# Sixteen-head attention on one core: the next head's incidence products are issued ahead of this head's scores below the diagonal

## The reference

```python
std_logits = jnp.einsum('bhqd,bhkd->bhqk', q, k) * scale
...
incidence = jnp.einsum('bqhp,bkhp->bhqk', read_lines, J_write)
decays = jax.nn.sigmoid(decay_logits)
...
weights = decays[:, None, None] ** diffs_pos[None] * past[None].astype(x.dtype)
bias = incidence * weights[None] * bias_scale[None, :, None, None]
logits = std_logits + bias
...
logits = jnp.where(causal_mask[None, None], -jnp.inf, logits)
attn = jax.nn.softmax(logits, axis=-1)
out = jnp.einsum('bhqk,bhkd->bqhd', attn, v).reshape(B, T, D)
```

## Time and profile before

| | |
|---|---|
| median of three runs | 1004.08 us (1004.01 to 1008.88) |
| the profiled execution | 1001.47 us, span 1000.2 us |
| mean granted TensorE clock | 0.949 |
| busy share of the span | PE 86%, PEld 53%, DVE 73%, ACT 66%, POOL 41% |
| chain of waits that ended last | PE 53%, DVE 8%, issue 3%, ACT 3% |
| first and last reduction of the maxima (L1821) | starts at 325.85 and 771.62 us |

### The profile page before, as it was taken

How to read it: one execution, slowest core, us unless ns; L and a number is a source line. 1 busy time by engine, 2 the same in 40 slices (tenths; PEclk the granted TensorE clock), 3 DMA queues, 4 the chain that set the end, 5 groups by cost and what they waited for, 6 DMA issues and landing times.

```text
span 1000.2 us, 25506 instructions
## 1 busy us (share of the span) xinstructions
PE 857.0 (86%) x9999; PEld 527.1 (53%) x9999; DVE 732.9 (73%) x1794; ACT 656.5 (66%) x1154; POOL 407.3 (41%) x667
## 2 busy tenths in 40 slices
PE   5688888876463799999999999999999759798997
PEld 3344455554342466666666666666666524443444
DVE  4776888888794787778787877778788366666654
ACT  4668888854442466767675676766676648585865
POOL 3043555446565565573655547364132210101001
PEclk9889999999786599999999999999999989999999
DMA  5000000000142252626335262633642000000000
GB/s 154 22 1 1 1 1 0 1 1 1 54 122 66 83 145 70 176 52 173 86 100 127 69 180 48 168 91 98 181 121 52 3 0 1 22 1 22 1 23 22
DMA packets 70698, 63.60 MB, mean 64 GB/s; under 512 B 30600, under 2 KB 62824, under 8 KB 70576
## 3 DMA queue, kind: packets, MB, share of 16 engines
q1 hardware_dynamic: 70064, 61.90, 23.4%
q10 hardware_dynamic: 512, 0.02, 0.0%
HBM read 34.02 MB, written 27.36 MB: 61 GB/s over the span
## 4 chain that ended last, share of the span: by engine, by line
PE 53%; DVE 8%; issue 3%; ACT 3%; POOL 0%; DVEq 0%; POOLq 0%; ACTq 0%
PE bank L2149 12%; PE bank L1727 8%; PE bank L1702 4%; PE bank L1675 4%; PE bank L1683 3%; PE bank L1664 3%; PE bank L1657 2%; PE bank L1667 2%; PE bank L1690 2%; PE bank L1693 2%; PE bank L1735 1%; ACT 4g L2207 1%; DVE bank L1811 1%; DVE 4f L2243 1%; DVE bank L1816 1%
## 5 line engine op out<-in xcount | busy, mean ns | idle before, releaser
L1891 ACT ACTIVATE ET<-bank 64x512 f32<-64x512 f32 x128 | 75.6, 591 | 114.4 <-PE bank L1693 113.3
L1816 DVE TENSOR_TENSOR bank<-bank,WT 128x256 f32<-128x256 f32 x128 | 55.2, 431 | 86.8 <-PE bank L1683 84.7
L2230 DVE TENSOR_TENSOR act<-4f,act 128x512 f16<-128x512 f32 x96 | 66.4, 691 | 57.7 <-ACT act L2197 57.5
L1886 ACT ACTIVATE ET<-bank 128x768 f32<-128x768 f32 x128 | 103.2, 807 | 3.3 <-PE bank L1702 0.9
L1727 PE MATMUL bank<-ET,vv 128*32 128x128 f32 (+2 forms) x1792 | 89.1, 323 | 0.8 <-DVE O L1846 0.8
L1821 DVE TENSOR_REDUCE mo<-bank 128x4 f32<-128x512 f32 x128 | 87.3, 682 | 1.1 <-PE bank L1667 0.9
L2197 ACT ACTIVATE act<-4f 128x512 f16<-128x512 f32 x96 | 60.4, 630 | 28.3 <-DVE 4f L2243 26.2
L1829 DVE TENSOR_REDUCE mo<-bank 128x3 f32<-128x384 f32 x128 | 69.9, 546 | 0.0
L1830 DVE TENSOR_REDUCE mo<-bank 128x3 f32<-128x384 f32 x128 | 69.9, 546 | 0.0
L1811 DVE TENSOR_TENSOR bank<-bank,W 128x256 f32<-128x256 f32 x128 | 54.3, 424 | 12.9 <-PE bank L1657 12.9
L2149 PE MATMUL bank<-act,std 128*128 128x512 f16 x256 | 58.2, 390 | 0.0
(11 more groups left out here) (385 smaller groups left out, 2531.1 us busy)
## 6 DMA issues: line engine op xcount, KB each, us to landing
ring<-scr_q SPq DMA_DIRECT2D x16, 324.0 KB
QO<-scr_q SPq DMA_DIRECT2D x16, 324.0 KB
ring<-scr_a SPq DMA_DIRECT2D x16, 252.0 KB
KA<-scr_a SPq DMA_DIRECT2D x16, 252.0 KB
ring<-scr_k SPq DMA_DIRECT2D x16, 168.0 KB
KB<-scr_k SPq DMA_DIRECT2D x16, 168.0 KB
scr_a<-dk SPq DMA_DIRECT2D x8, 288.0 KB, 4.5
X<-in_x SPq DMA_DIRECT2D x8, 256.0 KB, 5.2
```

Source lines behind the costliest of these rows:

```text
L1816: dve.tensor_tensor(half(psDT, 0), half(psDT, 0), over(WT[:, h * HB:(h + 1) * HB], NT), ALU.mult).then_inc(s_wk, 1)
L1886: act.activation(ET[n % NE][:, T:SEG * P], psXT[:, 0:NP * P], ACT.Exp).then_inc(s_expo, 1)
L1891: act.activation(to[0:HB, :], psDT[0:HB, :], ACT.Exp)
L2230: dve.tensor_tensor(lo, f32_[f % 3], hi, ALU.subtract).then_inc(s_lo, 1)
```

## The change

In TensorE's loop, the call for the incidences of head n+1 is put ahead of the call for the scores below the diagonal of head n. The other four engines' streams are the same, instruction for instruction. Both steps keep their waits and their buffers.

```diff
                 if 0 <= j < HEADS:
                     incidences_by_key(j)
+                if n + 1 < HEADS:
+                    incidences(n + 1)
                 if n < HEADS:
                     below(n)
-                if n + 1 < HEADS:
-                    incidences(n + 1)
                 if 0 <= j < HEADS:
                     on_diagonal_by_key(j)
```

## The result

The changed kernel takes 1009.59 us, the median of six runs (1006.08 to 1010.7), against 1004.05 us for the kernel before in six runs (1002.89 to 1008.88). The ratio is 1.0042, with a 95% interval of 1.0022 to 1.0062. So it is slower, by 4.2 us going by the ratio, which lies just inside the 5 us called "no change". The profiled execution took 1006.08 us with a span of 1004.8, which is 4.6 more than before. +5.3 us and 1009.4 us were forecast.

What follows compares the result with a forecast made beforehand. TensorE was taken to set the pace, VectorE close in a few heads. 2.4 + 0.6 + 0.9 + 0.4 + 1.0 = 5.3 us on 1001.47 gives 1006.8, plus a 2.6 offset 1009.4 us; 8-in-10 range 1004 to 1014.

Steps and rivals of the forecast that it cites:

- The likeliest case: Whole kernel: late maxima now hold up TensorE's scores below and all behind them, +5.3 us; chance 0.57.
- Heads 4 in each 16: Seven heads where the wait for late maxima loses its cover: 0.34 us late each, 2.4 us.
- Heads 8: Five heads, 8 in each 16, whose maxima end late: 0.12 us each, 0.6 us.
- Heads 12: Nine heads, 12 in each 16: earlier incidences end the weighting's wait, yet maxima stay late; 0.1 us each, 0.9 us.
- The other losses: Last 17 heads: five more with late maxima, about 0.1 us each; 0.4 us after what the next wait covers.
- An undisturbed round: Round without late maxima, such as head 53: 0.85 us from L1683 to L1690 in either order.
- One step between 64 and 128 columns more or less: Rival on TensorE's column changes per round: one less gives 1000 us (chance 0.04), one more 1019 us (0.03).
- Absorbed or not: Rival: lost pieces are caught up at the next wait for the weighting; +2.2 us, 1006.3 us, chance 0.18.
- the term of the first eight heads: Low-clock start: scores below wait for the maxima, +0.3 us at head 4, +0.7 at head 7; sum 1.0, bounds 0 to 5.
- The rule weighed: Weight loads pulled past the waiting matmul would save some 0.08 us at each of 21 stops; not taken into the sum.
- the profile's total for the late maxima: Expected sign: L1657's load waits for L1821 some 4 us in about 15 places, up from 2.1 us in 11.
- The chance of a gain: Rival: earlier incidences end the weighting's 5.4 us of waits in 300 us, saving 8 us; 996 us, chance 0.06.

Runs made afterwards that it cites:

- Both moves: Incidences first on TensorE, plus VectorE's weighting moved up right behind the weighting by key, against the kernel before: ratio 1.0003 in all rounds.

## Why the prediction was right, point by point

- **The likeliest case came true, in place and size.** The steady part was forecast as 2.4 + 0.6 + 0.9 + 0.4 = 4.3 us, and 4.18 is measured from head 12 to head 127. Heads 4 in each 16: 0.34 us in seven heads, as forecast. Heads 8: 0.13 (forecast 0.12). Heads 12: 0.08 in each of nine (forecast 0.1). The other losses, in the last 17 heads, make the rest, 0.4 us; heads 116 and 124 were covered as said, and so was head 55, whose maxima came 0.2 us late and not 0.1 (1.04 from L1683 to L1690), at no cost to the round.
- **An undisturbed round stayed as it was**, 0.84 for 0.85 us. One step between 64 and 128 columns more or less would have shown in every round. The rule of the Trainium skill in "TensorEngine Tiling (Array Packing)", "Key Properties", that a change of tiling mode and not of the tile is what drains, agrees with that: the number of changes was the same, four in a round.
- **Absorbed or not:** nothing of the steady loss was caught up later but where the prediction said so. In the rounds after a late one all starts keep the same shift to the hundredth.
- **The step that failed is the term of the first eight heads.** Forecast +1.0 us, measured -0.65 up to head 12 in both profiles of the changed kernel, at a clock of 0.71 for 0.57 over the first eight. Its two parts were right at an equal clock: +0.3 us for head 4 (0.3 in heads 4 and 5) and +0.7 for head 7 (0.6). It left out the gain of 0.5 us in the round of head 0, though VectorE was said to be the last to finish there, and the small losses of heads 1 and 2, 0.25 us together, weren't covered by head 3. Above all it held the clock fixed or lower, where the new order kept it up for longer.
- **Luck in the total.** 1009.4 us forecast and 1009.59 measured agree to 0.2 us, but the sum was 5.3 for a timed 4.2, and its 1.0 us for the first heads wasn't there in the profiles. The offset of 2.6 us between the profiled execution and the median is no property of the kernel: for the changed kernel it is 3.5.
- **The rule weighed** (in the Trainium skill, page "TensorE: Matmul & The Clock Gate", section "The mechanism": weight loads are pulled ahead of matmuls in flight): in head 52 after the change the load of L1657 again starts with its matmul, after 0.53 us of idle, and L1675 follows by the full 0.25. So across this wait the trace doesn't show it. The steady sum by the row, 4.3 us, held at 4.18; the one by the rule would have been 1.7 us lower.
- **Not as I said:** the profile's total for the late maxima. I expected 4 us in 15 places, and it shows 2.6 in 5, since the losses of 0.1 us in heads 8 and 12 aren't marked as waits. The per-round times show them, the summary doesn't.
- **The chance of a gain** went with the weighting of VectorE. The wait that the change removes (5.4 us) lay in rounds where TensorE didn't need the weighting yet. Where TensorE did wait for it, side work stood in front, and the change doesn't move that. Both moves in all rounds gave the loss back (406.39 us from head 12 on), and with every fourth round left out they gained 4.1 us there. The early weighting alone lost 0.67; with the group maxima moved too the old order gained 2.2.

## What to carry to other kernels

An operation that is moved up takes its wait along, and everything that stood ahead of it now stands behind that wait: look for the rounds in which the wait was covered by the work it passes, and count those rather than the average. In a loop whose side work repeats, the order can be chosen per round: the same two moves give 1.0003 of the time before when made in all rounds and 0.9944 when every fourth is left out. To send a result early is worth something if the engine that takes it has it next in its own queue, as VectorE had in the round of head 0 (0.5 us), and here was worth nothing where side work stood in front.

## What the runs showed of the hardware

The steady stretch of 115 heads, at a clock of 1.00, lies between 406.34 and 406.43 us in four profiles of kernels that have the old order there, while whole executions of the kernel before lie between 1000.71 and 1008.95 us, and two of one and the same kernel took 998.88 and 1004.96. In the thirteen profiles the spread is outside that stretch: the start of head 0 lay between 324.6 and 332.3 us, with the same instructions ahead of it, and the clock was low for 59 to 82 us of that time. The two that started last had the most of it (82 us), but of five with 61.5 or 61.6 us four started at 324.6 to 325.0 and one at 330.4, so the clock isn't the only cause.

In the first eight heads, where TensorE is partly idle, the same work took 26.69 us at a clock of 0.50 and 24.38 at 0.71 in two executions of one kernel. And a small change of order moved the clock: with 0.5 us less in the round of head 0 it was still at 1.00 in the round of head 2 (five executions), and at 0.51 to 0.54 without (six).
